# Moving the first output projection of an attention and feed-forward kernel into its last attention units

## The chip, the cores and the metric

The kernel runs on one core of a Trainium2 chip. The time is that of one execution on the device, in microseconds (us). Each core has a matrix engine (TensorE, PE in the profile, with its weight loads as PEld), a vector engine (VectorE, DVE), a scalar engine (ScalarE, ACT), a general engine (GpSimd, POOL) and SyncE (SP), which here issues nearly all DMA transfers. Each engine works through its own instructions in order and waits on semaphores for the others.

## What is computed

One cross-attention layer and one feed-forward layer with ternary weights, each added to its input. Cut to what matters:

```
x  = x + attn(layernorm(x), ctx)          # x 16x100x512, ctx 16x361x256
  q = rmsnorm(x Wq), k = rmsnorm(ctx Wk), v = ctx Wv     # 16 heads of 128
  o = softmax(q k' / sqrt(128)) v
  attn = o Wo                             # Wo 2048x512
x  = x + ffn(layernorm(x))
  bitlinear(a, w): a = fwht(a) (Hadamard), per row rounded to 8-bit integers by its
      absolute maximum; w rounded to -1, 0, 1 times its mean magnitude; a w'
  gate, up = bitlinear(h, w_gate), bitlinear(h, w_up)    # 512 to 2048
  ffn = bitlinear(silu(gate) * up, w_down)               # 2048 to 512
```

## The kernel before

Products that need more than one fp32r pass are made from split operands: a matrix a is written as hi (a rounded to fp32r) and lo (a - hi), and three products hi*hi, hi*lo, lo*hi are summed in PSUM. ACT makes the hi part, DVE the lo part.

**queries** makes q for all tokens, in four groups of 400 tokens. Per group the normed x is transposed into four PSUM banks (psX), split into xT_hi and xT_lo (one buffer each), and each of the 16 heads h is twelve products into psQ[h % 2]. ACT reads each head twice (q_out, squares). xT of the next group is split at head 15 (high_xT on ACT, low_xT on DVE). Wq arrives in four pieces of 1 MB through two staging slots, split where SPLIT_AT says. The middle groups are a loop.

**attention** works in 64 units (16 batches, 4 heads each); units 61 to 63 have no keys left to make, since keys run 12 heads ahead. In a unit TensorE does, for h = 0 to 3, the scores of a head (psS), and in between the transposes of two heads' probabilities pr (psP, line 778), the gather psZ of two units' contexts, and at h = 2 the values product of two units earlier (line 803). The softmax chain of a head is psS, DVE's scaling with maximum (line 1030) and nb (1037), ACT's exponential (875), DVE's inverse sum ri (1019), ACT's pr (882). The factors of the keys, rk, go by DMA to POOL and back, a unit or two ahead (spread_rk on SP, rms on POOL). Two units run on after the last (64 and 65) to finish gathers and values. The first half of Wo, 8 heads, is loaded in units 60 and 62 into four small slots and split by POOL in units 62 and 63 into wk_hi and wk_lo, whose keys are done (split_wo). o of the first 128 tokens is loaded into o_in at unit 60.

**feed_forward** works on 13 tiles of 128 tokens. Its steps are a pipeline: step(i) does gate and up of tile i + 1, the projection's end and the norm of tile i + 2, and down of tile i. Step -2 is the first. Per tile: out_proj (16 heads of three products, into psA), the residual sum, norm and first half of the Hadamard rotation on DVE (xn, xr), TensorE's transposes (norm_T), xT split, rotate_in, scales, rounding (mag, q), q1_T, gate_up, silu and product on ACT and DVE (stage), rotations, hidden_T, rotate_hidden, rounding, a DMA transpose, and down. Before the first step ACT and DVE split o of tile 0 and the second half of Wo (high_wo; L1527, L1550), and TensorE does out_proj(0), the last heads of it behind the v_w semaphore. busy(bank, n) issues n products whose results nobody uses. Heads 0 to AHEAD - 1 (6) of the projection of tile t + 1 are done ahead of gate_up of tile t. The feed-forward weights (wt, 3 MB, already ternary) are loaded by SP behind Wo's second half, x, had and o of tile 1. At the end, y is a scaling by ACT (scale_down) and an addition by POOL (result).

## Time and profile before

| | |
|---|---|
| median of three runs | 1473.45 us (1469.47 to 1475.27) |
| the profiled execution | 1468.72 us, span 1466.8 us |
| PE busy | 1427.9 us, 97% of the span |
| PEld busy | 1225.7 us, 84% |
| DVE busy | 954.2 us, 65% |
| ACT busy | 947.1 us, 65% |
| POOL busy | 524.0 us, 36% |
| queries, attention | about 0 to 188, 188 to 1048 us |
| feed-forward | about 1049 to 1467 us |

The profile is of one execution. Its timeline lists the instructions of an engine with start, length, and, where the engine stood idle before one, how long and what ended that. A matmul's length is modelled and overlaps the next, so the distance of two starts is what one costs in a row of many. A wait on several semaphores is put down to the one that came last.

### The profile page before, as it was taken

To read this page: it belongs to the slowest core of one execution; us is meant where nothing else is said; L and a number is where in the kernel's file an instruction comes from. 1 tells how busy PE (TensorE), PEld (TensorE's weight loads), DVE (VectorE), ACT (ScalarE), POOL (GpSimd) and SP (SyncE) were. 2 spreads that over 40 slices of the span, in tenths; PEclk is the share of its full clock that TensorE was granted. 3 is DMA by queue.
4 is the path that set the end of the run, shared out by engine and by line. 5 is a ranking of instruction groups with operands and counts; after the bars stand their busy time and mean duration, and the time that the engine had idled before them with its cause. 6 is when DMAs were issued, how large, how long until landed. Compare 5 with 4: busy or idle time off the path is not lost. (4 is left out here: it accounts for less than half of the span.)

```text
span 1466.8 us, 30515 instructions
## 1 busy us (share of the span) xinstructions
PE 1427.9 (97%) x8997; PEld 1225.7 (84%) x8997; DVE 954.2 (65%) x2464; ACT 947.1 (65%) x2069; POOL 524.0 (36%) x323
## 2 busy tenths in 40 slices
PE   8999989999999999999999999999899999999998
PEld 8888868999999989989999999998767677767765
DVE  5312056677777777777777777766467677767774
ACT  4556568878888878888788888887433334333432
POOL 0033324433322233323332333334244555555533
PEclk9999999999999999999999999999999999999999
DMA  7767723343444434343344434335533222322211
GB/s 238 215 180 195 206 78 85 103 110 106 116 125 117 120 105 116 112 130 110 106 122 124 115 110 115 105 83 140 158 118 88 71 57 64 95 69 57 64 32 40
DMA packets 187783, 165.07 MB, mean 113 GB/s; under 512 B 111040, under 2 KB 162256, under 8 KB 185872
## 3 DMA queue, kind: packets, MB, share of 16 engines
q1 hardware_dynamic: 180752, 151.21, 37.7%
q10 hardware_dynamic: 6912, 12.59, 2.7%
q8 instruction: 36, 0.59, 0.2%
q14 instruction: 83, 0.68, 0.2%
HBM read 123.44 MB, written 33.14 MB: 107 GB/s over the span
## 5 line engine op out<-in xcount | busy, mean ns | idle before, releaser
L707 POOL TENSOR_TENSOR rk_sp<-ms_sp,neg_half 76x10 f32<-76x10 f32 (+1 forms) x128 | 244.2, 1925 | 594.0 <-DMA ms_sp<-ms 594.0
L1030 DVE CUSTOM_DVE_ANT_0 sc<-psS,rk 100x361 f32<-100x361 f32 x256 | 136.3, 532 | 106.6 <-PE psS L765 82.9
L882 ACT ACTIVATE pr<-ex,ri 100x361 f32<-100x361 f32 x256 | 152.8, 597 | 81.5 <-DVE ri L1019 81.3
L875 ACT ACTIVATE ex<-sc,nb,rq 100x361 f32<-100x361 f32 x256 | 175.2, 684 | 8.5 <-DVE nb L1037 8.4
L741 PE MATMUL psK<-cT_hi,wk_hi 128*128 128x362 f32 x512 | 169.9, 332 | 1.7 <-DVE k_lo L1000 1.7
L863 ACT ACTIVATE k_hi<-psK 128x362 fp32r<-128x362 f32 x256 | 120.8, 472 | 76.1 <-PE psK L741 75.0
L741 PE MATMUL psK<-cT_lo,wk_hi 128*128 128x362 f32 x512 | 167.7, 328 | 0.0
L741 PE MATMUL psK<-cT_hi,wk_lo 128*128 128x362 f32 x512 | 167.7, 328 | 0.0
L1000 DVE TENSOR_TENSOR k_lo<-psK,k_hi 128x362 fp32r<-128x362 f32 x256 | 134.4, 525 | 6.7 <-ACT sq L869 5.4
L790 PE MATMUL psZ<-pT_hi,cK_hi 120*128 120x400 f32 (+1 forms) x384 | 132.8, 346 | 0.0
L790 PE MATMUL psZ<-pT_hi,cK_lo 120*128 120x400 f32 (+1 forms) x384 | 132.3, 344 | 0.0
L790 PE MATMUL psZ<-pT_lo,cK_hi 120*128 120x400 f32 (+1 forms) x384 | 132.3, 344 | 0.0
L803 PE MATMUL psNV<-z,wv_sb 128*128 128x100 f32 x1024 | 124.9, 275 | 1.4 <-issue 1.4
L803 PEld LDWEIGHTS psNV<-z,wv_sb 128*128 128x128 f32 x1024 | 119.4, 192 | 2.0 <-issue 2.0
L778 PEld LDWEIGHTS psP<-ident,pr 100*120 100x120 f32 (+1 forms) x768 | 79.7, 165 | 49.2 <-issue 27.7
L869 ACT ACTIVATE sq<-psK 128x362 f32<-128x362 f32 x256 | 118.7, 464 | 0.0
L778 PE MATMUL psP<-ident,pr 100*120 100x100 f32 (+1 forms) x768 | 96.9, 262 | 8.3 <-ACT pr L882 8.1
L1011 DVE TENSOR_TENSOR pT_lo<-psP,pT_hi 121x600 fp32r<-121x600 f32 x128 | 99.0, 774 | 4.2 <-ACT pT_hi L890 3.0
L741 PEld LDWEIGHTS psK<-cT_hi,wk_hi 128*128 128x128 f32 x512 | 96.5, 188 | 6.3 <-DVE k_lo L1000 5.1
L329 PE MATMUL psQ<-xT_hi,wq_hi 128*128 128x400 f32 x256 | 90.9, 355 | 7.0 <-ACT sq L406 5.9
L1019 DVE RECIPROCAL ri<-rs 100x1 f32<-100x1 f32 x256 | 41.3, 161 | 86.0 <-ACT ex L875 74.7
L1454 ACT ACTIVATE hT_hi<-psT 128x512 fp32r<-128x512 f32 x52 | 29.7, 596 | 104.4 <-PE psT L1364 104.4
(177 smaller groups left out, 3582.9 us busy)
## 6 DMA issues: line engine op xcount, KB each, us to landing
rk<-rk_dram SPq DMA_DIRECT2D x64, 564.1 KB
o_in<-o_dram SPq DMA_DIRECT2D x13, 1024.0 KB, 6.0
q_dram<-q_out SPq DMA_DIRECT2D x64, 200.0 KB, 4.4
q_in<-q_dram SPq DMA_DIRECT2D x64, 200.0 KB, 4.9
o_dram<-o SPq DMA_DIRECT2D x64, 200.0 KB, 5.3
stage<-in_w_ff SPq DMA_DIRECT2D x12, 1024.0 KB, 6.7
w_in<-in_w_ff ACTq DMA_DIRECT2D x48, 256.0 KB, 3.1
cT_in<-in_ctxT SPq DMA_DIRECT2D x16, 361.0 KB, 5.0
```

The lines of the kernel that those rows point to most:

```text
L707: nc.gpsimd.tensor_tensor(rk_sp[:, cols], ms_sp[:, cols], neg_half[0:HG * SKR, :].to_broadcast([HG * SKR, n]), op=ALU.pow).then_inc(g_rk, 1)
L741: last = nc.tensor.matmul(psK[h % 2][:, 0:SKP], w[:, c, col:col + D], x[:, slot, c, :], start=(n == 0), stop=(n == 3 * CC - 1))
L778: last = nc.tensor.transpose(psP[0:KW[i], k, i * SQ:(i + 1) * SQ], pr[:, 2 * half + k, KO[i]:KO[i] + KW[i]], ident[0:SQ, 0:SQ])
L790: last = nc.tensor.matmul(psZ[c][:, 0:UQ], w[0:KW[i], slot, i, c * P:(c + 1) * P], x[0:KW[i], j % 2, i, :], start=(n == 0), stop=(n == 8))
L803: last = nc.tensor.matmul(psNV[:, h * SQ:(h + 1) * SQ], wv_sb[:, c, col:col + D], z[:, j % 2, c, h * SQ:(h + 1) * SQ], start=(c == 0), sto ...
L863: nc.scalar.activation(k_hi[:, j, h, :], psK[h % 2][:, 0:SKP], ACT.Copy)
L869: nc.scalar.activation(sq[:, j % 2, h, :], psK[h % 2][:, 0:SKP], ACT.Square).then_inc(a_k, 1)
L875: nc.scalar.activation(ex[:, h % 2, :], sc[:, h % 2, :], ACT.Exp, bias=nb[:, h % 2:h % 2 + 1], scale=rq[:, j % 2, h:h + 1], accum_out=rs[: ...
L882: nc.scalar.activation(pr[:, h, :], ex[:, h % 2, :], ACT.Copy, scale=ri[:, h % 2:h % 2 + 1]).then_inc(a_pr, 1)
L1000: nc.vector.tensor_tensor(k_lo[:, j, h, :], psK[h % 2][:, 0:SKP], k_hi[:, j, h, :].bitcast(F32), ALU.subtract).then_inc(v_klo, 1)
L1011: nc.vector.tensor_tensor(two_heads(pT_lo, j, half), psP[0:KW[0], :, 0:3 * SQ].rearrange("p k (i q) -> p k i q", q=SQ), two_heads(pT_hi, j ...
L1030: nc.vector.tensor_tensor_reduce(out=sc[:, h % 2, :], in0=psS[0:SQ, 0:SK], in1=rk[:, j % 2, h, :], scale=1.0, scalar=-3.0e38, op0=ALU.mult ...
```

## The change

1. The projection of tile 0 moves out of the feed-forward stage into attention units 62 to 65, into psK's first bank, which becomes a bank that all stages share (bank0, psA afterwards). o of tile 0 is split there in four parts (high_o on ACT, low_o on DVE, unit 62) into the storage of cT and a new tile.
2. All of Wo is loaded and split in the attention stage. Heads 0 to 7 go to wk_hi and wk_lo, by POOL, from unit 61 on; heads 8 to 15 go to the keys' ring (ring_hi, ring_lo, whose storage is the keys' of attention and part of the queries' Wq and xT), hi by ACT in units 63 to 65, lo by POOL. There are nine slots, five of them in sq. On SP, o_in, x of tile 0 and the first four loads of Wo now stand ahead of unit 62's q and factors; five more stand between the two halves of unit 63's factors. o of tile 1 is loaded at unit 63.
3. The feed-forward stage starts with the residual of tile 0. Step -2 on TensorE interleaves heads 0 to 9 (FIRST) of tile 1's projection with tile 0's norm_T, rotate_in and q1_T; the 27 + 5 fillers there go. The weights' DMAs stand behind had and x of tile 1. Tile 0's transposes go to psT[0].
4. At the end, down of tile 11 moves ahead of the fillers, which are 13 for 27, and the last result is one DVE instruction, with no moving of residuals behind it.
5. In the queries, xT has two buffers and is split at heads 12 and 15; Wq's second piece is split at head 1 for head 0; the group loops are written out.

The diff, cut to its core:

```diff
-        SPLIT_AT = {0: 1, 2: 2, 4: 3, 8: 4, 10: 5}
+        SPLIT_AT = {1: 1, 2: 2, 4: 3, 8: 4, 10: 5}
+        XT_AT = {12: (0, 1), 15: (2, 3)}
...
-            with act.Fori(1, G - 1) as g:
+            for g in range(1, G - 1):
...
+        WO_HI_AT = {(UNITS - 3, 1): range(0, 4), **{(UNITS - 2, h): (4 + h,) for h in range(HG)}}
+        WO_LO_AT = {(UNITS - 1 + i // HG, i % HG): (8 + i,) for i in range(H // 2)}
+        WO_ACT_AT = {(UNITS - 1, 0): (8,), (UNITS - 1, 1): (9,), (UNITS - 1, 2): (10, 11), (UNITS - 1, 3): (12,),
+                     (UNITS, 0): (13,), (UNITS, 1): (14,), (UNITS, 2): (15,)}
+        OUT_AT = {(UNITS - 2, 0): (0,), (UNITS - 2, 2): (1, 2), (UNITS - 1, 0): (3,), (UNITS - 1, 1): (4, 5), (UNITS - 1, 2): (6, 7),
+                  (UNITS, 0): (8, 9), (UNITS, 1): (10,), (UNITS, 2): (11, 12), (UNITS + 1, 1): (13,), (UNITS + 1, 2): (14, 15)}
+        O_PARTS = [(0, 4), (4, 8), (8, 11), (11, H)]
...
+                if isinstance(u, int) and u == UNITS - 1:
+                    sp.wait_ge(p_ss, UNITS)
+                    for i in range(4, 9):
+                        load_wo(i)
                 sp.wait_ge(g_rk, powers)
...
+            def first_out(h):
+
+                if h == 0:
+                    pe.wait_ge(a_k, HEADS)
+                    pe.wait_ge(v_klo, HEADS)
+                part = [k for k, (lo, hi) in enumerate(O_PARTS) if lo <= h < hi][0]
+                pe.wait_ge(v_of, part + 1)
+                pe.wait_ge(g_wlo, h + 1)
+                o_hi, o_lo = (p[part][:, h - O_PARTS[part][0], :] for p in o_parts)
+                hi, lo = (w[h // 8][:, h % 8, :] for w in (wo_hi, wo_lo))
+                for i, (w, m) in enumerate(((o_hi, hi), (o_hi, lo), (o_lo, hi))):
+                    nc.tensor.matmul(psK[0][:], w, m, start=(h == 0 and i == 0), stop=(h == H - 1 and i == 2))
...
-            for i in range(PIECES):
-                sp.dma_start(slots[i].rearrange("p (h n) -> p h n", h=2), wo_v[PIECES + i]).then_inc(d_wo[i], 16)
-            sp.dma_start(x_in[:], x[0:TT, :]).then_inc(d_x, 16)
             sp.dma_start(stage[:, 1, 0:HC * HB].rearrange("p (c n) -> p c n", c=HC), had_in.rearrange("(c p) n -> p c n", p=P)
                          ).then_inc(d_had, 16)
-            for i in range(2):
-                sp.wait_ge(d_stored[i], 16 * B * NG // 2)
-            load_o(1, TT)
+            load_x(1, TT)
             for w in range(3):
                 sp.dma_start(wt[:, w, :, :].bitcast(BF16), wt_dram[w * WC:(w + 1) * WC].rearrange("c p n -> p c n")
                              ).then_inc(d_wt, 16)
...
             def step(i):
+                if isinstance(i, int) and i == -2:
+                    out_proj(1, range(0, 3))
+                    norm_T(0)
+                    out_proj(1, range(3, 5))
+                    rotate_in(0)
+                    out_proj(1, range(5, 9))
+                    q1_T(0)
+                    out_proj(1, range(9, FIRST))
+                    return
...
-                if isinstance(i, int) and i == TILES - 2:
-                    busy(psA, 27)
+                late = isinstance(i, int) and i == TILES - 2
+                if late:
+                    down(i, 0, front)
+                    down(i, 1, front)
+                    busy(psA, 13)
...
-            busy(psT[0], 6)
+            busy(psT[1], 8)
             pe.wait_ge(v_ident, 1)
-            out_proj(0, range(0, AHEAD))
...
+            def last_result(t):
+
+                dve.wait_ge(p_down, t + 1)
+                dve.wait_ge(d_out, t * 16)
+                dve.wait_ge(g_old, (t + 2) * 2)
+                dve.wait_ge(v_scale[1], 5 * t + 5)
+                nc.vector.scalar_tensor_tensor(y[:], psF[:], ald[:], x1[:, 0, :], ALU.mult, ALU.add).then_inc(v_y, 1)
```

TensorE in unit 62, from a head's scores (psS2) to the next head's, before:

```order
L765 MATMUL psS2<-k_hi,q_hi 100x362
L765 MATMUL psS2<-k_lo,q_hi 100x362
L765 MATMUL psS2<-k_hi,q_lo 100x362
L778 MATMUL psP<-ident,pr 121x100
L778 MATMUL psP<-ident,pr 120x100 x2
```

and after; the new rows' names are those of the storage, wk for Wo and cT for o:

```order
L814 MATMUL psS2<-ring_lo,q_hi 100x362
L814 MATMUL psS2<-ring_hi,q_lo 100x362
L867 MATMUL bank0<-wk_hi,cT_hi 128x512
L867 MATMUL bank0<-wk_lo,cT_hi 128x512
L867 MATMUL bank0<-wk_hi,cT_lo 128x512
L827 MATMUL psP<-ident,pr 121x100
L827 MATMUL psP<-ident,pr 120x100 x2
```

One head of the projection stands between the scores and the transposes of pr.

DVE from the start of the feed-forward stage to the rotated norm of tile 0, before:

```order
L1541 CAST ident_b<-ident 128x128
L1545 TENSOR_TENSOR o_lo<-o_in,o_hi 128x512 x4
L1550 TENSOR_TENSOR wo_lo<-stage,wo_hi 128x1024 x2
L1550 TENSOR_TENSOR wo_lo<-mag,wo_hi 128x1024 x2
L1555 CAST had<-stage 128x512
L1571 TENSOR_TENSOR x<-psA,x_in 128x512
L1573 BN_STATS st<-x 128x6
L1576 BN_AGGR mv<-st 128x2
L1578 TENSOR_SCALAR ve<-mv 128x1
L1695 TENSOR_TENSOR o_lo<-o_in,o_hi 128x2048
L1584 TENSOR_SCALAR xn<-x,mv,rstd 128x512
L1592 TENSOR_TENSOR xr<-xn 128x256 x2
```

and after:

```order
L1631 CAST ident_b<-ident 128x128
L1658 TENSOR_TENSOR x<-bank,x_in 128x512
L1660 BN_STATS st<-x 128x6
L1663 BN_AGGR mv<-st 128x2
L1665 TENSOR_SCALAR ve<-mv 128x1
L1635 TENSOR_TENSOR o_lo<-o_in,o_hi 128x512 x2
L1671 TENSOR_SCALAR xn<-x,mv,rstd 128x512
L1679 TENSOR_TENSOR xr<-xn 128x256 x2
L1640 CAST had<-stage 128x512
L1635 TENSOR_TENSOR o_lo<-o_in,o_hi 128x512 x2
L1683 TENSOR_TENSOR xT_lo<-psT,xT_hi 128x512
```

Nine instructions stood ahead of the statistics' end, five do now; two of tile 1's four o_lo pieces stand between the statistics and the norm, two and had's rounding behind it.

TensorE behind the last tile's projection, from gate_up (psB<-wt) on, before:

```order
L1352 MATMUL psB<-wt,q1T 128x512 x32
L1392 MATMUL psA<-wk_hi 128x512 x27
L1364 MATMUL psT0<-ident,stage3 128x128 x4
L1364 MATMUL psT1<-ident,stage3 128x128 x4
L1384 MATMUL psF<-wt,q2T 128x512 x16
```

and after:

```order
L1445 MATMUL psB<-wt,q1T 128x512 x32
L1477 MATMUL psF<-wt,q2T 128x512 x16
L1485 MATMUL bank0<-wk_hi 128x512 x13
L1457 MATMUL psT0<-ident,stage3 128x128 x4
L1457 MATMUL psT1<-ident,stage3 128x128 x4
```

Down (psF) of tile 11 went from behind the transposes of the hidden tile to ahead of the fillers.

## Rows read from the trace of the kernel before

**Rows 1.** Windows: us, busy time (instructions) of PE, PEld, DVE, ACT, POOL, clock, DMA:

```profile
1077.90:1434.90 357.00, 352.27 (x1931) 247.74 (x1930) 257.78 (x483) 135.63 (x181) 190.83 (x120) 1.00 0.26 63
```

**Rows 2.** Timeline, queries: start, length, engine, line, operation, [idle before, what ended it]:

```profile
26.24 1.92 ACT L363 ACTIVATE wq_hi<-stage 128x2048 fp32r<-128x2048 f32 x1 [1.05 <-DMA stage<-in_wq]
...
100.13 0.42 PE L329 MATMUL psQ<-xT_hi,wq_hi 128*128 128x400 f32 x1 [0.57 <-DVE xT_lo L469]
...
142.07 0.42 PE L329 MATMUL psQ<-xT_hi,wq_hi 128*128 128x400 f32 x1 [0.52 <-issue]
```

**Rows 3.** Timeline of PE, units 62 to 65: transposes of pr, last values product:

```profile
1016.34 0.80 PE L778 MATMUL psP<-ident,pr 100*121 100x100 f32 x6 [0.52 <-ACT pr L882]
...
1020.71 0.80 PE L778 MATMUL psP<-ident,pr 100*121 100x100 f32 x6 [0.96 <-ACT pr L882]
...
1036.55 0.80 PE L778 MATMUL psP<-ident,pr 100*121 100x100 f32 x6 [1.04 <-ACT pr L882]
...
1045.78 2.00 PE L803 MATMUL psNV<-z,wv_sb 128*128 128x100 f32 x16 [0.71 <-issue]
```

**Rows 4.** Timeline of PE, first and 24th product of the projection of tile 0:

```profile
1050.93 0.47 PE L1305 MATMUL psA<-wk_hi,o_hi 128*128 128x512 f32 x1
...
1056.23 0.39 PE L1305 MATMUL psA<-wk_hi,o_lo 128*128 128x512 f32 x1
```

**Rows 5.** Timeline, DVE in unit 62; ACT and DVE splitting o later:

```profile
1016.72 0.21 DVE L1037 TENSOR_SCALAR nb<-mx,rq 100x1 f32<-100x1 f32 x1
...
1049.31 2.20 ACT L1533 ACTIVATE o_hi<-o_in 128x512 fp32r<-128x512 f32 x4 [1.00 <-PEq L527]
...
1049.98 2.50 DVE L1545 TENSOR_TENSOR o_lo<-o_in,o_hi 128x512 fp32r<-128x512 f32 x4
```

**Rows 6.** Timeline, POOL at unit 63's factors; DVE and ACT beside POOL's split:

```profile
1015.47 3.70 POOL L707 TENSOR_TENSOR rk_sp<-ms_sp,neg_half 76x10 f32<-76x10 f32 x2 [11.38 <-DMA ms_sp<-ms]
...
1021.11 0.96 DVE L993 TENSOR_TENSOR q_lo<-q_in,q_hi 128x400 fp32r<-128x400 f32 x1
1022.00 1.23 DVE L995 COPY rq<-rq_all 100x4 f32<-100x4 f32 x1
...
1023.32 0.60 ACT L882 ACTIVATE pr<-ex,ri 100x361 f32<-100x361 f32 x1 [1.31 <-DVE ri L1019]
```

**Rows 7.** Timeline, first feed-forward step, chain from the residual to gate_up:

```profile
1063.38 0.69 DVE L1571 TENSOR_TENSOR x<-psA,x_in 128x512 f32<-128x512 f32 x1 [1.35 <-PE psA L1305]
...
1065.48 0.55 POOL L1233 TENSOR_TENSOR rstd<-ve,neg_half 128x1 f32<-128x1 f32 x1 [14.80 <-DVE ve L1578]
...
1066.23 2.51 DVE L1695 TENSOR_TENSOR o_lo<-o_in,o_hi 128x2048 fp32r<-128x2048 f32 x1 [0.90 <-ACT o_hi L1447]
...
1070.35 0.66 PE L1313 MATMUL psA<-ident,xr 128*128 128x128 f32 x4 [0.88 <-DVE xr L1592]
...
1071.67 0.69 DVE L1596 TENSOR_TENSOR xT_lo<-psA,xT_hi 128x512 fp32r<-128x512 f32 x1 [1.38 <-ACT xT_hi L1461]
...
1077.91 7.23 PE L1352 MATMUL psB<-wt,q1T 128*128 128x512 fp8e4 x32
```

**Rows 8.** Windows, as rows 1, while the feed-forward weights were loading:

```profile
1060.00:1065.00 5.00, 5.00 (x23) 3.79 (x22) 3.29 (x6) 2.52 (x4) 0.00 (x0) 1.00 1.12 336
```

**Rows 9.** Timeline, second step: DVE's sum across halves, PE's hidden transposes:

```profile
1090.54 1.22 DVE L1680 TENSOR_TENSOR stage<-stage 128x1024 f32<-128x1024 f32 x1
...
1091.82 1.09 PE L1364 MATMUL psT<-ident,stage 128*128 128x128 f32 x8
```

**Rows 10.** Timeline of the end: down, rotation, first hT_lo pair, last addition:

```profile
1442.84 3.62 PE L1384 MATMUL psF<-wt,q2T 128*128 128x512 fp8e4 x16
...
1446.11 0.47 PE L1374 MATMUL psB<-had,hT_hi 128*128 128x256 f32 x1
...
1443.24 1.29 DVE L1559 TENSOR_TENSOR hT_lo<-psT,hT_hi 128x512 fp32r<-128x512 f32 x2 [1.38 <-ACT hT_hi L1454]
...
1463.08 1.26 POOL L1272 TENSOR_TENSOR y<-y,x 128x512 f32<-128x512 f32 x1 [12.94 <-ACT y L1487]
```

More of the change, by code:

```diff
@@ L268, in _ @@
             group(0, True, False)
-            with pool.Fori(1, G - 1) as g:
+            for g in range(1, G - 1):
                 group(g, False, False)
@@ L346, in _ @@
             group(0, True, False)
-            with pe.Fori(1, G - 1) as g:
+            for g in range(1, G - 1):
                 group(g, False, False)
             group(G - 1, False, True)
-            busy(psX[0], wq_hi[:, 0, 0:P], xT_hi[:, 0, :], 4)
+            busy(psX[0], wq_hi[1][:, 0, 0:P], xT_hi[0][:, 0, :], 4)
             squares(G - 1, NG - 1)
-            busy(psX[0], wq_hi[:, 0, 0:P], xT_hi[:, 0, :], 6)
+            busy(psX[0], wq_hi[1][:, 0, 0:P], xT_hi[0][:, 0, :], 6)
             factors(G - 1)
@@ L496, in _ @@
             split_first(0)
-            low_xT(0)
+            for c in range(DC):
+                low_xT(0, c)
             split_first(1)
             group(0, True, False)
-            with dve.Fori(1, G - 1) as g:
+            for g in range(1, G - 1):
                 group(g, False, False)
@@ L1205, in _ @@
                              ).then_inc(d_wt, 16)
-            load_x(1, TT)
+            for i in range(2):
+                sp.wait_ge(d_stored[i], 16 * B * NG // 2)
             load_o(2, 2 * TT)
@@ L1407, in step @@
                     busy(psA, 27)
-                if real(i):
+                if real(i) and not late:
                     down(i, 0, front)
@@ L1508, in step @@
                     high_o(i + 3)
[L1509 removed]
+                if real(i) and not last_tile(i):
                     scale_down(i)
@@ L1541, in _, with low_o @@
             nc.vector.tensor_copy(ident_b[:], ident[:]).then_inc(v_ident, 1)
-            for k in range(NO):
+            def low_o(k):
                 heads = slice(k * OH, (k + 1) * OH)
@@ L1692, in step @@
                     residual(i + 2)
-                if isinstance(i, int) and i == -2:
-                    dve.wait_ge(a_o, NO + 1)
-                    nc.vector.tensor_tensor(o_lo[:], o_in[:], o_hi[:].bitcast(F32), ALU.subtract).then_inc(v_o, 1)
+                first = isinstance(i, int) and i == -2
+                if first:
+                    low_o(0)
+                    low_o(1)
                 if real(i + 1):
```

282 lines of the change are left out of this document (162 added, 120 removed).

## Prediction

> **What bounds the kernel now.** I read the stretches first. In the feed-forward stage TensorE is busy 352.27 of 357.00 us at full clock [rows 1], and the stages before it look alike, so TensorE's own order of work sets the time nearly everywhere. A gain can only come from places where TensorE waits, or does work that counts for nothing. The timeline of TensorE shows three such places. In the queries a few short waits remain [rows 2]. In the last attention units the keys are finished, and TensorE waits for the softmax chain before each turn of the probabilities and before each values product [rows 3]. The largest is the seam between attention and feed-forward: the last values product starts at 1045.78 and runs 2.00 us, the first useful product of the next stage starts at 1050.93 [rows 3, 4], and the first gate and up product at 1077.91 [rows 7]. The 27 us between these two are the projection of tile 0 followed by a chain of small steps with only fillers beside it. At the end of the kernel 27 fillers stand ahead of the last but one down (the order in the part on the change), which the chain then passes [rows 10].
>
> **Queries.** Splitting xT in two places with two buffers removes the wait for DVE xT_lo, 0.57 us, and written-out loops remove the one that nothing in the profile explains, 0.52 us [rows 2]. A loss is possible: the split of Wq's second piece moves behind the first head's two reads on ACT, about 1 us, so the DMA of the fourth piece goes out later; before, ACT got it at 26.24 after a wait for that DMA [rows 2]. The loss is nothing if the queue stays full and at most the moved split's own stretch, 2 to 3 us, if it passes through whole. The timeline lists no wait of TensorE right behind the 26.24 split, so I take 0.4: **-0.7**, bounds -1.5 and +1.5.
>
> **Last attention units.** The projection of tile 0, 16 heads of three products, is now done here. From 1050.93 to 1056.23 there are 23 starts, 0.23 us each [rows 4], so a head costs 0.69 us and all 16 cost 11.0. The heads stand ahead of five probability turns and two values products. The waits there are 0.52 (twice, the other 0.55), 0.96 (twice, the other 0.93), 1.04 and 0.71 (twice) [rows 3]. A product's modelled length overlaps the next by about 0.17, so the seven waits can hold 5.4 + 1.2 = 6.6 us. Filling without any loss costs 11.0 - 6.6 = 4.4 us.
>
> It isn't perfect. The first head in unit 62 needs the first four heads of o split. ACT can start that when the probabilities are done that let the turn begin at 1016.34 [rows 3], and takes a quarter of 2.20; DVE gets to it after its factor at 1016.72 + 0.21 = 1016.9 and takes a quarter of 2.50 [rows 5]. So the head starts near 1017.6, and the turn begins near 1018.25, 1.9 us late. Walking the other slots (0.3, 0.0, 1.4, 0.3, 0.2, 0.7, 0.5, 0.7 and 0.5 us: heads less the wait that they fill; two slots stand at no wait) adds 4.6: +6.5. ACT's five later splits and POOL's 24 Wo operations have the time of two units more than before and stay beside this.
>
> There is a price for the parts of o and Wo that run together. In unit 62, DVE's q_lo took 0.96 and the copy of rq, four elements, 1.23 us beside POOL's split, and ACT then waited 1.31 us for the inverse sum [rows 6]. Three of the four new o_lo pieces fall in the same company. An o_lo piece of 0.62 hides under the exponential; stretched by as much as that wait it doesn't. The bounds are nothing (before, that wait moved no turn: from 1016.34 to 1036.55 two units took 10.1 us each [rows 3]) and 3 x 1.3 = 3.9. I take 0.5, nearer to the case in which the wait was absorbed. **Attention +7.0**, bounds +4.4 and +10.4.
>
> The Trainium skill, SBUF — State Buffer, section "Who interferes with whom", says that a VectorE instruction with two SBUF inputs and a GpSimd one that reads SBUF exclude each other, and the later one waits for the whole of the other. By it each o_lo piece could meet a Wo split and lose the whole of that, and the term would be the upper bound above; by the row it is the 0.5. The stretched q_lo agrees with the rule.
>
> **Start of the feed-forward.** Let t be its first instant (1049.3 before, 1.5 us after the last values product ends). DVE is free about 0.7 later and adds x at once, since the projection is in the bank. From that add to POOL's power took 1065.48 - 1063.38 = 2.1, the power 0.55 [rows 7]: t + 3.4. Two o_lo pieces (1.25) end at t + 4.0 and cover most of the power. Norm and half rotation took 1.6 (o_lo's end, 1066.23 + 2.51, to TensorE's turn at 1070.35) [rows 7]: t + 5.6. TensorE's three heads of tile 1 start when the first o_lo piece is there and end at t + 5.4, just in time. xT_lo followed the turn by 1.32 [rows 7], t + 6.9, but now stands behind the rounding of had and two more pieces (1.7), t + 7.3. From xT_lo to gate_up took 6.24, of which 0.6 was TensorE still at heads of tile 1 [rows 7]. So gate_up is ready near t + 13.0 where it was t + 28.6: **-15.6**.
>
> Gate_up also needs all three of the ff weights' DMAs. They go out after the load of x for tile 1, which waits for the add: t + 1.4 and later. Had, x and the weights are 3.6 MB; at the 336 GB/s of the stretch in which they ran before [rows 8] that is 10.7 us, and with about 1.5 us to start t + 13.5. **+0.5**, bounds 0 (the chain is later anyway) and, at a rate a third lower, +5.
>
> Four heads more of tile 1 (2.8 us) are done before gate_up than before. I count nothing for them: in the next step TensorE's turn of the hidden tile, at 1091.82, starts as DVE's sum across halves ends, 1090.54 + 1.22 [rows 9]. TensorE will be early there and wait. From there on the tiles run as before.
>
> **End.** Down for tile 11 moves before 13 fillers in place of after 27. It takes 3.3 (1442.84 to 1446.11 [rows 10]) and 13 fillers 3.0, so TensorE, done with the last gate_up at the end of the stretch of [rows 1], 1434.9, is through at 1441.2, and the hidden turn before 1442.84 stays where DVE's sum puts it. The rotation at 1446.11 then waits only for the first hT_lo, 1443.24 + 0.65 = 1443.9 [rows 10]: -2.2. The last result is one DVE pass in place of an ACT pass and POOL's add of 1.26 [rows 10]: -1.2. The last stretch is all one chain, so both count: **-3.4**, bounds -2.2 and -3.6.
>
> **Sum.** -0.7 + 7.0 - 15.6 + 0.5 - 3.4 = **-12.2 us**. The profiled execution took 1468.7, its span 1466.8; the sum makes it 1456.5. The median of the three runs is 1473.45, 4.7 above that execution, and I take the difference as it stands: **1461.2 us**. The best ends together give -18, the worst -1; added as independent errors they leave about -17 to -6.
>
> **Rivals.**
> First, the seam moves rather than closes (chance 0.17): the heads in the units fill nothing, since ACT, with some 5 us more in units 62 and 63, is late at each turn by what TensorE was late before, and the weights' DMAs land late. Then attention costs its 10.4 and the weights 3 more than I took: -6.2, 1467.3. For it speaks that ACT waits under 1.4 us at a time in these units [rows 6]; against it that TensorE is pushed back by 7 us, and ACT with it.
> Second, exclusion on the last units (0.04), which would make the kernel **slower**. POOL's 24 operations on Wo now lie in units 61 to 64, beside four o_lo pieces, and the probabilities' chain passes DVE at every head. Each meeting that lands on the chain costs what the inverse sum lost, about 1.1 us [rows 6]. If all 24 did, it would be +26 us and the time near 1487; it decides from the twelfth meeting on. Before, 16 operations ran there and one was seen to cost this, and it was absorbed.
> Third, the first projection waits for its Wo (0.04): 24 operations, four of them ahead of the keys' factors for unit 63, push those factors late by about their length, 7.7 us. The loss would be some 5 us, 1466. Against it: before, POOL began the same factors at 1015.47, after 11.38 us of waiting for their DMA [rows 6], and the four pieces end at about that instant.
> Fourth, the edits gain more than I say (0.10): no loss in the queries, waits filled whole and the weights early: -17, 1456.
>
> **How the numbers follow.** The forecast itself has 0.65. Its own range is 1456 to 1466; with the spread of the medians (the three runs lie 6 us apart) and the first and fourth rivals, 1453.5 to 1468.5 leaves out two in ten. A measurement of this kernel tells about 0.5%, 7.4 us, from no change, so faster begins below 1466.1. The forecast and the fourth rival lie there but for their upper edge, the first and third lie half on either side or beyond: faster 0.79, same 0.16, slower 0.05.
>
> **What would show it.** Right: the last values product starts some 7 us later than 1045.78 (less the queries' gain), and the waits of [rows 3] are gone but one before the first head in unit 62; gate_up of tile 0 stands about 13 us behind the stage's start, with no long wait for a DMA before it; in the next step TensorE waits 2 to 3 us more for DVE before the hidden turn; from the first gate_up to the end of the last it is 357 us as before [rows 1]; from the last gate_up to the end it is 3.4 us shorter. Wrong: a first head near 1020 or later; gate_up waiting for the weights by several us; tiles that take longer; new waits for the keys' factors at units 62 or 63; or a loss in the first group of queries above 1.5 us.

## The result and the profile after

| | before | after |
|---|---|---|
| median | 1473.2 us (6 runs, 1469.47 to 1475.27) | 1464.6 us (6 runs, 1461.03 to 1465.72) |
| ratio, with 95% interval | | 0.9942 (0.9926 to 0.9959) |
| the profiled execution, its span | 1468.72, 1466.8 us | 1464.46, 1462.7 us |
| PE busy | 1427.9 us | 1422.4 us |

The change makes the kernel 8.6 us faster, 0.58% (by the interval 0.4 to 0.7%). The two profiled executions lie only 4.3 us apart, because that of before lies below all six timed ones and that of after at the median.

The timeline of after, TensorE: the first head of the projection in unit 62, a turn in unit 63, the last values product, the first product of tile 1's projection, the normed tile's turn and the first gate and up product. They answer to [rows 3], [rows 4] and [rows 7].

```profile
1019.31 0.47 PE L867 MATMUL bank<-wk_hi,cT_hi 128*128 128x512 f32 x1 [1.97 <-DVE cT_lo L1095]
...
1031.69 0.80 PE L827 MATMUL psP<-ident,pr 100*121 100x100 f32 x6 [1.21 <-ACT pr L946]
...
1055.12 1.92 PE L852 MATMUL psNV<-z,wv_sb 128*128 128x100 f32 x16
...
1061.63 0.47 PE L1398 MATMUL bank<-wk_hi,o_hi 128*128 128x512 f32 x1 [0.92 <-DVE o_lo L1635]
...
1064.10 0.66 PE L1406 MATMUL psT<-ident,xr 128*128 128x128 f32 x4
...
1073.46 4.87 PE L1445 MATMUL psB<-wt,q1T 128*128 128x512 fp8e4 x14 [2.27 <-DMA wt<-wt_dram]
```

The last values product starts 9.3 us later than in [rows 3] and gate_up 4.5 us earlier than in [rows 7]. The feed-forward stage begins at t = 1058.60; gate_up stands at t + 14.9 where it stood at t + 28.6. Ahead of gate_up TensorE waits 2.27 us for the weights.

The second step, which answers to [rows 9]: TensorE's hidden turn and the first rotated product.

```profile
1089.04 1.09 PE L1457 MATMUL psT<-ident,stage 128*128 128x128 f32 x8 [2.49 <-DVE stage L1767]
...
1091.48 0.58 PE L1467 MATMUL psB<-had,hT_hi 128*128 128x256 f32 x1 [1.35 <-DVE hT_lo L1644]
```

What the prediction didn't have is in the granted clock. Windows of after: us, busy time (instructions) of PE, PEld, DVE, ACT, POOL, clock, DMA. The first answers to [rows 1]; the next show both first feed-forward steps, the last two the start of the queries.

```profile
1073.40:1434.40 361.00, 354.50 (x1917) 249.06 (x1918) 258.44 (x483) 135.32 (x181) 190.72 (x120) 0.99 0.26 64
1072.00:1074.00 2.00, 0.54 (x2) 0.28 (x3) 0.00 (x0) 0.00 (x0) 0.00 (x0) 0.92 1.20 300
1074.00:1076.00 2.00, 2.00 (x6) 0.75 (x5) 0.00 (x0) 0.00 (x0) 0.00 (x0) 0.50 0.60 142
...
1092.00:1094.00 2.00, 2.00 (x12) 2.00 (x11) 1.97 (x5) 0.62 (x1) 0.75 (x1) 0.50 0.00 0
1094.00:1096.00 2.00, 2.00 (x11) 2.00 (x11) 0.99 (x2) 0.60 (x1) 2.00 (x1) 0.50 0.00 0
...
12.00:14.00 2.00, 2.00 (x13) 2.00 (x12) 1.82 (x3) 2.00 (x6) 0.00 (x0) 0.53 0.44 162
14.00:16.00 2.00, 2.00 (x14) 2.00 (x13) 2.00 (x4) 0.77 (x1) 0.00 (x0) 0.62 0.00 0
```

Three times the clock falls from its upper level (1.00, 2.4 GHz) to the lower (0.50, 1.2 GHz), each time right behind idle time of TensorE: 2.27 us at 1071 to 1073, then 2.49 and 1.35 us around the hidden turn (the transposes of the hidden tile), and 1.91 us at 8.4 to 10.3 ahead of the first transposes of x. Gate_up of tile 0 takes 8.55 us (1073.46 to 1082.01) where before took 6.88 (1077.91 to 1084.79); from the hidden turn to the next gate_up it is 15.84 us for 14.34. From the first gate_up to the end of the last it is 361 us, not 357.

The end, from the chain that ended last (start, length, what; the x27 are fillers, L1477 is down, L1775 the new last result), with the span's end at 1462.7:

```profile
1449.06 6.17 PE bank L1485 x27
1455.22 0.60 issue
1455.82 3.63 PE psF L1477 x16
1459.45 0.02 issue
1459.47 0.75 DVE y L1775
```

From the last gate_up, 1427.48, to the end it is 35.2 us; before, from 1428.04 to 1466.8, it was 38.8.

### The profile page after: what moved, and what is told of

Same layout as the page of the kernel before. It is cut to its first block and busy times, and to the rows that moved or that the text cites. A ratio compares the mean times of both kernels' runs of the same rounds, so it can differ in the third digit from the quotient of the medians.

```text
span 1462.7 us, 30158 instructions
## 1 busy us (share of the span) xinstructions
PE 1422.4 (97%) x8953; PEld 1223.1 (84%) x8953; DVE 951.7 (65%) x2464; ACT 947.3 (65%) x2075; POOL 528.6 (36%) x328
## 5 line engine op out<-in xcount | busy, mean ns | idle before, releaser
L1445 PE MATMUL psB<-wt,q1T 128*128 128x512 fp8e4 x416 | 95.7, 384 | 3.2 <-DMA wt<-wt_dram 2.3
L814 PE MATMUL psS<-ring_hi,q_hi 128*100 128x362 f32 x256 | 92.0, 359 | 4.6 <-DVE mx L1119 4.6
L927 ACT ACTIVATE ring_hi<-bank 128x362 fp32r<-128x362 f32 x128 | 60.2, 470 | 50.2 <-PE bank L790 50.2
L1445 PEld LDWEIGHTS psB<-wt,q1T 128*128 128x128 bf16 x416 | 38.9, 98 | 57.2 <-issue 18.1
L790 PE MATMUL bank<-cT_hi,wk_hi 128*128 128x362 f32 x256 | 85.3, 333 | 1.0 <-DVE ring_lo L1082 1.0
L790 PE MATMUL psK<-cT_hi,wk_hi 128*128 128x362 f32 x256 | 85.0, 332 | 0.6 <-DVE ring_lo L1082 0.6
L968 ACT ACTIVATE pT_hi<-psP 121x600 fp32r<-121x600 f32 x128 | 83.9, 655 | 0.7 <-PE psP L827 0.6
L814 PE MATMUL psS<-ring_lo,q_hi 128*100 128x362 f32 x256 | 84.1, 329 | 0.0
```

Of the source, the lines that this page charges most:

```text
L790: last = nc.tensor.matmul(psK[h % 2][:, 0:SKP], w[:, c, col:col + D], x[:, slot, c, :], start=(n == 0), stop=(n == 3 * CC - 1))
L814: last = nc.tensor.matmul(psS[0:SQ, 0:SKP], w[:, j % 2, cols], x[:, j, h, :], start=(i == 0), stop=(i == 2))
L968: nc.scalar.activation(two_heads(pT_hi, j, half), psP[0:KW[0], :, 0:3 * SQ].rearrange("p k (i q) -> p k i q", q=SQ), ACT.Copy).then_inc(a_ ...
L1445: last = nc.tensor.matmul(psB[:, 2 * (j % 2) + k, :], q1T[:, c, :], wt[:, k, c, j * DIM:(j + 1) * DIM], start=(c == 0), stop=(c == DC - 1))
```

## The experiments

All traces in one table, each number a difference of two starts in one trace's timeline. "Head 0" is the start of the first q_out in the queries; "0 to 6" the distance of the seventh's to it; "61 to 62" and "61 to 65" the distances between the values products in those units (V61 is the one in unit 61, V62 the next, and so on); "V to G" from the last of these (V65) to the first gate_up (G0); "G0 to G1" and "G1 to G12" between the gate_ups of tiles 0, 1 and 12; "end" from that of tile 12 to the end of the span. Times are us; "clock" is the mean granted clock of the traced execution. Each ratio below is to the kernel before, executed beside it (medians 1469.51, 1471.32 and 1470.09 us). E4_no_heads and e9_gates were executed once and have none.

| kernel | head 0 | 0 to 6 | 61 to 62 | 61 to 65 | V to G | G0 to G1 | G1 to G12 | end | clock |
|---|---|---|---|---|---|---|---|---|---|
| before | 16.36 | 18.28 | 10.13 | 34.57 | 32.13 | 28.25 | 321.88 | 38.8 | 0.999 |
| b1_before | 16.71 | 17.87 | 10.12 | 34.60 | 31.96 | 28.24 | 321.86 | 38.7 | 0.999 |
| after | 18.45 | 20.59 | 12.43 | 42.37 | 18.34 | 31.42 | 322.60 | 35.2 | 0.995 |
| a2_after | 17.64 | 20.14 | 13.97 | 43.93 | 18.42 | 31.26 | 323.26 | 35.2 | 0.993 |
| e1_fillers | 17.83 | 20.23 | 12.50 | 42.53 | 18.92 | 28.14 | 322.84 | 35.2 | 0.998 |
| e2_tail_undone | 16.74 | 20.33 | 12.45 | 42.44 | 19.24 | 29.70 | 322.59 | 37.5 | 0.996 |
| e3_split_at_0 | 16.40 | 17.70 | 13.99 | 42.98 | 17.02 | 28.71 | 322.75 | 35.2 | 0.998 |
| e4_no_heads | 21.05 | 20.34 | 13.54 | 40.66 | 18.06 | 28.77 | 322.89 | 35.2 | 0.993 |
| e5_weights_first | 16.42 | 20.30 | 13.34 | 43.52 | 16.29 | 29.16 | 322.76 | 35.2 | 0.998 |
| e6_pool_gate | 17.00 | 20.43 | 12.44 | 42.17 | 17.92 | 30.18 | 322.63 | 35.1 | 0.998 |
| e7_head_moved | 16.72 | 20.08 | 11.84 | 41.98 | 18.03 | 28.81 | 323.27 | 35.2 | 0.996 |
| e9_gates | 16.26 | 20.10 | 14.49 | 43.50 | 19.12 | 31.01 | 322.68 | 35.2 | 0.994 |
| c1_all | 16.16 | 17.92 | 14.01 | 43.69 | 16.04 | 28.19 | 322.86 | 35.2 | 0.999 |
| c2_all | 17.69 | 17.96 | 10.99 | 41.02 | 16.55 | 28.10 | 322.25 | 35.1 | 1.000 |

**The kernel before once more** (no edit).

> The kernel before, unchanged, profiled again. The one profiled execution of before lies 4.7 us below the median of its three runs, and its granted clock was 0.999 where all six runs of the changed kernel show 0.994 to 0.996. In the changed kernel's trace the opening fillers of TensorE end at 8.35, it idles 1.91 us and the clock is 0.50 from about 12 to 15.5; in before's trace they end at 9.31, it idles 0.51 and the clock stays at 1.00. Theory: which of the two happens at the start changes from run to run in either kernel and is worth 2 us (first head's q_out at 16.36 or near 18.4); then most of these executions have a clock below 0.999 and are 2 us or more above 1468.7. Rival: the start is the changed kernel's own doing; then every execution of before shows 0.999 and the first head at 16.4.

Its ten runs have a median of 1468.77 us, ratio 0.9997 (0.9987 to 1.0006), clocks of 0.998 to 1.000; the thirteen of before beside them have 0.997 to 1.000. The new trace shows 1.72 us of idle time ahead of the first transposes and still a clock of 1.00 with head 0 at 16.71. So neither theory holds as it stands: the fall at the start stands in neither trace of before, but it isn't the changed kernel's own doing either, since in six of the eight variants below that leave the start as it is head 0 stands between 16.26 and 17.00. The mean granted clock of all executions tells the two apart: 0.9955 over the six of a2_after, 0.9990 over the eleven of before beside it. By estimate that is 0.0035 of 1461 us, 5.1 us of TensorE's work lost, some of it under waits.

**Fillers in the first two steps.** The first line stands at the end of step -2, ahead of the first gate_up, the others around the hidden turn.

```diff
+                    busy(psF, 10)
...
+                if isinstance(i, int) and i == -1:
+                    busy(psF, 13)
                 if real(i + 1):
                     hidden_T(i + 1, 0)
                     hidden_T(i + 1, 1)
+                if isinstance(i, int) and i == -1:
+                    busy(psF, 6)
```

> The changed kernel with products whose results nobody uses in the places where TensorE stood idle in the first two feed-forward steps: 10 ahead of the first gate_up, 13 ahead of the hidden turn and 6 behind it in the second step. Theory: the idle stretches made the granted clock fall to 0.50 from 1073.9 to 1076.5 and from 1091 to 1097, which cost gate_up 8.55 in place of 6.88 us (1.7) and the rotations 15.84 in place of 14.34 us (1.5); with fillers both are back and the kernel is 3.2 us faster. Rival: the chains on DVE set these stretches and the clock only fills their waits: no change. Second rival: the fillers end later than the data and cost up to 1 us.

Windows of e1_fillers, with the columns of those above, over gate_up and over the second step:

```profile
1071.00:1079.00 8.00, 7.44 (x35) 3.37 (x35) 2.52 (x4) 2.12 (x4) 2.09 (x2) 1.00 0.25 60
1083.00:1099.00 16.00, 15.32 (x99) 13.20 (x98) 13.57 (x31) 6.65 (x9) 9.70 (x5) 1.00 0.27 73
```

The clock stays at 1.00 and G0 to G1 is 28.14 us, as before the change, for 31.42: the theory holds in the trace, to the 3.3 us. The ratio, 0.9945 (0.9928 to 0.9961), shows nothing of it: the medians don't bear the gain out. The weights landed late in this trace (15.4 us behind the stage's start, V to G 18.92), and the spread of the other stretches is as large as the gain. The second rival has a small part: the 13 fillers reach past the end of DVE's sum at 1085.50, and the hidden turn starts at 1085.82, 0.3 behind it. The stretch is as short in c1_all and c2_all (28.19 and 28.10), the kernels in which the same fillers stand around the hidden turn.

**The end undone.**

```diff
                 if late:
-                    down(i, 0, front)
-                    down(i, 1, front)
-                    busy(psA, 13)
+                    busy(psA, 27)
```

> The changed kernel with down of tile 11 again behind the turn of the hidden tile and 27 fillers ahead, as in before; the single-pass last result stays. By the prediction this gives back 2.2 us of the 3.4 at the end. Rival: the order is hidden behind the chain on DVE and only the single pass counted; then the end is as long as before this edit and the time is the same.

The end is 37.5 us, 2.3 more than with the edit (35.2) and 1.3 less than before (38.8). That is the prediction's 2.2 and 1.2. The ratio, 0.9946 (0.9930 to 0.9963), is too coarse for it.

**Wq's second piece split ahead of the first head.**

```diff
-        SPLIT_AT = {1: 1, 2: 2, 4: 3, 8: 4, 10: 5}
+        SPLIT_AT = {0: 1, 2: 2, 4: 3, 8: 4, 10: 5}
```

> The changed kernel with the second piece of Wq split ahead of the first head again, as in before. By the prediction the later split costs 0.4 us (bounds 0 and 2 to 3). By the traces the first group lost another 2.0 us between its second and its seventh head (q_out of head 6 at 39.04, 4.4 later than before, of which 2.1 are the clock at the start): if the later split is the cause, this kernel's head 6 stands 2.3 us or less behind before's and the kernel gains up to 2 us. Rival: the loss is in the stores of q that share the queue with the loads, and the place of the split is worth under 0.5.

ACT in the first group, timeline of after and then of e3_split_at_0: the split of Wq's fourth piece and the q_out of head 6.

```profile
29.02 1.91 ACT L369 ACTIVATE wq_hi<-stage 128x2048 fp32r<-128x2048 f32 x1 [3.00 <-DMA stage<-in_wq]
...
39.04 0.59 ACT L405 ACTIVATE q_out<-bank,gprod 128x400 f32<-128x400 f32 x1 [2.80 <-DMA q_dram<-q_out]
```

```profile
25.23 1.92 ACT L369 ACTIVATE wq_hi<-stage 128x2048 fp32r<-128x2048 f32 x1 [0.49 <-DMA stage<-in_wq]
...
34.10 0.60 ACT L405 ACTIVATE q_out<-bank,gprod 128x400 f32<-128x400 f32 x1 [3.06 <-PE psQ L337]
```

From head 0 to head 6 it is 17.70 us, and 17.9 in the other two kernels with this line, for 20.1 to 20.6 in the nine with the later split: 2.4 us. The ratio is 0.9923 (0.9906 to 0.9940), with that of e5_weights_first the lowest of the single edits, though its interval overlaps that of after. The later split frees the staging slot later, the fourth piece lands later, and its split stands ahead of q_out on ACT. Measured from head 0, the second piece's split ends 3.0 us later in after than in e3_split_at_0, and 2.4 of these come through to head 6.

**The projection's products left out.** Only the last head's first product stays; the waits for o and Wo stay too.

```diff
-                for i, (w, m) in enumerate(((o_hi, hi), (o_hi, lo), (o_lo, hi))):
-                    nc.tensor.matmul(psK[0][:], w, m, start=(h == 0 and i == 0), stop=(h == H - 1 and i == 2))
+                if h == H - 1:
+                    nc.tensor.matmul(psK[0][:], o_hi, hi, start=True, stop=True)
```

> The changed kernel without the products of the first output projection in attention units 62 to 65 but for one, so the first tile's result is wrong. All splits of o and Wo stay. Theory: TensorE's own extra work is what the last values product is late by (it starts 60.4 us after the one of unit 57 at 994.7 in the changed kernel, 7.8 us more than before); then the last units are as short as before within 0.5 us. Rival: the splits on ACT, DVE and POOL hold up the chain of the probabilities; then 1 us or more of the 7.8 stays without the products.

TensorE's timeline in units 62 and 63:

```profile
1021.98 1.36 PE L827 MATMUL psP<-ident,pr 100*121 100x100 f32 x6 [2.42 <-DVE cT_lo L1095]
...
1027.88 0.77 PE L827 MATMUL psP<-ident,pr 100*121 100x100 f32 x6 [1.06 <-ACT pr L946]
...
1035.29 1.28 PE L827 MATMUL psP<-ident,pr 100*121 100x100 f32 x6 [2.18 <-ACT pr L946]
```

Without 47 of the 48 products units 61 to 65 still take 40.66 us, 6.1 more than before. The rival wins in the first two units: from V61 to V63 it is 25.99 us, 20.22 before and 25.53 in after, so there the arrival of o_lo and of the probabilities holds TensorE up and the products only fill that time. From V63 to V65 the theory holds: 14.67 us, 14.35 before and 16.84 in after, so there the products cost 2.2 of the 2.5 us. Part of the 6.1 is the clock: the two turns of 1.36 and 1.28 us took 0.80 in [rows 3], behind 2.42 and 2.18 us of idle time. At the 1.5 us that such a fall costs in c1_all below, the two are at most 3 us of it (an estimate). So this run overstates what the splits alone cost, and the share of each stays open.

**The weights ahead of x.**

```diff
-            load_x(1, TT)
             for w in range(3):
                 sp.dma_start(wt[:, w, :, :].bitcast(BF16), wt_dram[w * WC:(w + 1) * WC].rearrange("c p n -> p c n")
                              ).then_inc(d_wt, 16)
+            load_x(1, TT)
```

> The changed kernel with the DMAs of the feed-forward weights ahead of the load of x for tile 1, which waits for the residual. Theory: the weights land 1.4 us earlier and more, since x no longer stands ahead; gate_up of tile 0, 14.9 to 15.8 us behind the stage's start in three traces, starts at 12.6 to 13.0, where the chain is ready; without the idle stretch the clock stays at 1.00 there: 2 to 4 us faster. Rival: the transfer rate sets it and the other loads of the start (o of tiles 2 and 3) share it: no change.

The first gate_up of this kernel:

```profile
1069.97 0.81 PE L1445 MATMUL psB<-wt,q1T 128*128 128x512 fp8e4 x3 [0.23 <-DMA wt<-wt_dram]
```

The first gate_up in TensorE's timeline stands 12.8 us behind the stage's start (1057.17) and waits 0.23 us; in the nine changed kernels with the old order it is 13.5 to 15.8 us. The clock is 1.00 throughout gate_up. The theory holds for this stretch. The ratio, 0.9924 (0.9907 to 0.9942), is some 2 to 2.5 us below those of after and a2_after, inside the theory's 2 to 4, but the intervals overlap.

**POOL held back once.**

```diff
+                if i == 6:
+                    pool.wait_ge(v_rq, UNITS)
```

> The changed kernel with POOL waiting, before its seventh piece of Wo, until DVE has q_lo and the copy of rq for the last unit. Theory: DVE's q_lo (0.98 us) and copy of four elements (1.25 us) in unit 62 are stretched by POOL's splits beside them, ACT's pr then waits 2.23 us for the inverse sum and TensorE's turn at 1031.69 waits 1.21 us; apart, they take 0.56 and 0.16, that turn comes about 1 us earlier, and the kernel is about 1 us faster. Rival: TensorE waits elsewhere instead, for Wo's seventh head that is split later: no change or up to 1 us slower.

In after, POOL's split, DVE's two instructions and ACT's pr in unit 62; they answer to [rows 6].

```profile
1026.35 1.50 POOL L762 TENSOR_TENSOR wk_lo<-sq,wk_hi 128x512 fp32r<-128x512 f32 x1
...
1025.72 0.98 DVE L1075 TENSOR_TENSOR q_lo<-q_in,q_hi 128x400 fp32r<-128x400 f32 x1
1026.62 1.25 DVE L1077 COPY rq<-rq_all 100x4 f32<-100x4 f32 x1
...
1027.98 0.60 ACT L946 ACTIVATE pr<-ex,ri 100x361 f32<-100x361 f32 x1 [2.23 <-DVE ri L1108]
```

In e6_pool_gate the same two of DVE, and the later piece of o_lo with POOL's split beside it:

```profile
1024.07 0.57 DVE L1077 TENSOR_TENSOR q_lo<-q_in,q_hi 128x400 fp32r<-128x400 f32 x1
1024.55 0.16 DVE L1079 COPY rq<-rq_all 100x4 f32<-100x4 f32 x1
...
1027.88 1.52 DVE L1097 TENSOR_TENSOR o_rest_lo<-o_in,o_rest_hi 128x640 fp32r<-128x640 f32 x1
...
1027.41 1.31 POOL L764 TENSOR_TENSOR wk_lo<-sq,wk_hi 128x512 fp32r<-128x512 f32 x1
```

The copy of four elements ends at 1027.87 where POOL's split ends at 1027.85, and takes 0.16 without it. The piece of o_lo ends at 1029.40, 0.68 behind POOL's 1028.72. So the stretch is one waiting for the other's end. The Trainium skill, SBUF — State Buffer, section "Who interferes with whom", says that a DVE instruction with two SBUF inputs contends with one of POOL that reads SBUF, and that a DVE copy does so in its two-port modes. The trace agrees for o_lo; which mode the copy of rq ran in it doesn't show. The stretch moved but wasn't removed: TensorE's wait in unit 63 went from 1.21 to 0.99 us, the ratio is 0.9944 (0.9927 to 0.9960). What holds that turn now is the same meeting one instruction later: the inverse sum stands behind the stretched o_lo on DVE, and ACT's pr waits 1.42 us for it.

```profile
1029.51 0.60 ACT L948 ACTIVATE pr<-ex,ri 100x361 f32<-100x361 f32 x1 [1.42 <-DVE ri L1110]
```

The rival is right for the time but not for its reason: no wait of TensorE for POOL's Wo stands in this timeline.

**All five together.** The three edits above, the fillers of the second step, and at the very start 29 fillers for 22 and 9 for 11.

```diff
-            busy(psQ[0], weights["ones"][:], weights["ones"][:], 22)
+            busy(psQ[0], weights["ones"][:], weights["ones"][:], 29)
```

> The changed kernel with five edits together: Wq's second piece split ahead of the first head, seven more fillers at the very start and two fewer behind the transposes, the feed-forward weights ahead of x, POOL's wait as in the run before, and fillers in the second feed-forward step around the hidden turn. If each does what its theory says: 3.0 for the split, up to 2 for the start (only in executions in which the clock fell there), 3 for the weights, 1 for POOL, 1.5 for the fillers, about 9 us below the changed kernel, ratio to before near 0.988. Rival: the gains overlap in the same waits, and it is not better than the changed kernel with the split alone, 0.9923.

Ratio 0.9899 (0.9883 to 0.9914), 1455.81 us beside 1471.32: 6 us better than after by the ratios, for the 9 hoped for. The trace shows one reason, TensorE's first head in unit 62 and the six transposes behind it:

```profile
1014.22 0.47 PE L869 MATMUL bank<-wk_hi,cT_hi 128*128 128x512 f32 x1 [1.96 <-DVE cT_lo L1097]
...
1014.99 1.10 PE L829 MATMUL psP<-ident,pr 100*121 100x100 f32 x6
```

The six took 0.80 us in [rows 3]. Behind 1.96 us of idle time the clock falls here too; its mean from 1010 to 1018 is 0.82, and units 61 to 62 take 14.01 us. The same wait in after (1.97) had no fall behind it and 12.43 us; in a2_after, the same kernel, it had one and 13.97 us. So one fall costs 1.5 us here, and whether it comes changes from execution to execution: of the ten traces with this wait five have it (a2_after, e3, e4, e9, c1_all) and five don't.

**The first head moved**, and **POOL held back three times**.

```diff
-        OUT_AT = {(UNITS - 2, 0): (0,), (UNITS - 2, 2): (1, 2),
+        OUT_AT = {(UNITS - 2, 2): (0, 1, 2),
```

> The changed kernel with the first head of the projection moved from unit 62's first place to its third (heads 0, 1 and 2 stand there together). In the changed kernel TensorE waits 1.97 us for DVE's cT_lo ahead of that head and does the turn behind it late; in two variants the clock also fell to 0.50 behind this wait (units 61 to 62 between values products: 14.0 in place of 12.4 us, before 10.1). Theory: without the wait the turn comes 2.2 us earlier, the third place costs 0.8 more, and the distance of the two values products is 11.0 to 11.3 with no fall of the clock: 1.2 us faster than without the fall, 2.8 than with it. Rival: the chain of the probabilities (ACT and DVE also split o there) is late by as much; then the distance stays at 12 or more.

```profile
1014.61 0.80 PE L827 MATMUL psP<-ident,pr 100*121 100x100 f32 x6 [0.51 <-ACT pr L946]
...
1020.71 0.80 PE L827 MATMUL psP<-ident,pr 100*121 100x100 f32 x6 [0.56 <-ACT pr L946]
```

The 1.97 us are gone, the turn waits 0.51 for pr, and units 61 to 62 take 11.84 us for 12.4 or 14.0. It is 0.5 to 0.8 more than the theory said, and those 0.56 us are a new wait for pr behind three heads: a part of cT_lo took 1.70 us in this trace. Ratio 0.9935 (0.9913 to 0.9957), not to be told from after's 0.9942.

```diff
+                if i in (5, 7):
+                    pool.wait_ge(v_of, {5: 2, 7: 4}[i])
+                if i == 6:
+                    pool.wait_ge(v_rq, UNITS)
```

> The changed kernel with three waits on POOL, so that each of its splits of Wo in unit 62 starts behind one of DVE's: the sixth piece behind the second part of o_lo, the seventh behind the copy of rq, the eighth behind the fourth part of o_lo. With the seventh alone held back, rq took 0.16 us and q_lo 0.57, but a part of cT_lo took 1.66 and o_rest_lo 1.49 beside other splits. Theory: it is the meeting of two instructions that stretches, wherever it falls; apart, all of these take 0.54 to 0.85, ACT's waits for the inverse sum of 1.4 to 2.2 us go, and units 61 to 63 (values product to values product, 12.4 + 13.1) shrink by 1 to 2 us. Rival: POOL, later by 2 to 3 us, makes the heads of the projection wait for Wo: they stay as long.

This one is inconclusive. Rq and q_lo took 0.15 and 0.56, but two parts of cT_lo still 1.13 and 1.32, and the first head waited 2.45 us with a fall of the clock behind it. ACT's longest wait for the inverse sum in unit 62 was 0.93 us for 2.23, and TensorE's wait in unit 63 was 0.29 us for 1.21, but it is 0.29 in e3_split_at_0 too, where the copy of rq took 1.25. Units 61 to 62 took 14.49, 62 to 63 12.19; the sum, 26.7 with one fall of the clock in it, is no better than after's 25.5 without one and near a2_after's 27.1 with one.

**The changed kernel again, and all edits.**

> The changed kernel, unchanged, on the same chip as the next run, for comparison: ratio to before 0.994.

> All edits of the combined kernel, with the three waits on POOL in place of one and with the first head moved to its third place. If both theories hold: 2.8 us for the head (in the combined kernel the clock fell behind that wait) and 1 to 2 for the waits, so some 4 us below the combined kernel, ratio to before 0.987, 10 us or more below the changed kernel. Rival: one stretch of the chain takes the place of the other, ratio 0.990 as before.

A2_after: 1461.81 us, ratio 0.9938 (0.9923 to 0.9953), clocks 0.993 to 0.998. C2_all: 1450.73 us beside 1470.09 for before on the same chip, **ratio 0.9870 (0.9853 to 0.9886)**, 19.4 us faster than before and 11.1 faster than the changed kernel. Windows of c2_all over the start, unit 62 and the first two feed-forward steps:

```profile
8.00:20.00 12.00, 10.12 (x76) 9.77 (x75) 9.74 (x19) 6.57 (x10) 1.03 (x1) 1.00 0.53 187
1010.00:1018.00 8.00, 7.49 (x47) 7.00 (x46) 5.43 (x17) 6.85 (x15) 7.62 (x8) 1.00 0.79 258
1066.00:1098.00 32.00, 30.98 (x167) 21.71 (x167) 21.91 (x41) 11.31 (x15) 14.98 (x9) 1.00 0.37 75
```

The clock never falls there, though TensorE waits 1.88 us ahead of the first transposes of x, and the four executions have 0.999 to 1.000. Units 61 to 62 take 10.99 us, 0.9 more than before with three heads in them. The three waits on POOL did not do their part: rq took 1.26 us again and ACT waited 2.23 us for the inverse sum, since POOL's sixth piece came just then. Its gate, the second part of o_lo, had been open since 1018.19, so it followed the fifth piece at 1019.98 with no wait; the gate held nothing back here. Of the 4.3 us over c1_all by the ratios, 2.7 stand in units 61 to 65, where the head was moved and the fall of the clock is gone.

## Why the prediction was right or wrong

The sign, the range and the place were right; the time was 1464.6 for 1461.2, a gain of 8.6 for 12.2. The mechanism was right too: the seam closes by more than the attention units grow. Two of the terms were too favourable, attention and tiles. The terms, by the means of all traces that leave a stretch as the change made it against the two of before:

| step | predicted | measured | how |
|---|---|---|---|
| Queries | -0.7 | -0.4 | head 0 +0.9, heads 0 to 6 +2.2, head 6 to the last q_out -3.5 |
| Attention | +7.0 | +9.1 | last q_out to V61 +0.7, V61 to V65 +8.4 (42.96 for 34.58) |
| Start, with the weights | -15.1 | -13.8 | V to G, 18.27 for 32.04 |
| Tiles | 0 | +2.6 | G0 to G1 +1.65, G1 to G12 +0.91 |
| End | -3.4 | -3.6 | 35.18 for 38.74 |
| Sum | -12.2 | -6.1 | the medians say -8.6 and -8.3 |

The traced executions of before lie 4.5 and 1.8 us below the medians of their runs. Those of the changed kernel and its variants lie on both sides: after's at the median, a2_after's the slowest of six, e1's and e3's the fastest of four. So the traces understate the gain by about 2 us. The terms are to be read with that.

Some figures of the prediction's working don't add up, though the forecast itself does. The best ends together give -16.3 and not -18, the first rival's terms -5.8 and not -6.2, and -17 to -6 from 1473.45 is 1456 to 1467 and not 1466. No run shows the 1.5 us that the weights' DMAs were given to start; what was measured is under Start.

**Queries.** The sum was near by luck, since two errors cancel. The moved split was put at 0.4 since no wait of TensorE stood right behind the 26.24 split; it costs 2.4, within the 2 to 3 us that the text gave as its whole length. The wait shows at head 4, as ACT's 3.00 us for the fourth piece, and at head 5, as its 3.36 us for stores of q. From head 6 to the last q_out it is 145.4 us for 148.9, 3.5 less where 1.09 was forecast. TensorE's idle time in that stretch went from 5.3 us in before to 2.0 in after, of which the prediction counted two waits. Of the edits the two buffers and the written-out loops act there; which of them brings it wasn't tried. No run ties head 0's +0.9 to an edit: it changes with how long TensorE waits for the first normed x (up to 3.63 us, in e4_no_heads) and with the fall of the clock there, and it is +0.5 without e4_no_heads.

**Attention.** The step that rested on o_lo was near: the turn behind the first head stands 2.2 us later behind V61 than in before (7.33 for 5.13) where 1.9 was said. The walk over the slots failed at unit 63, where a wait of 1.21 us for pr stayed at 1031.69. The meeting of DVE and POOL, priced at 0.5, stands ahead of it: ACT's pr of 1027.98 is 2.23 us late, and ACT then works with a pause of 0.23 us up to the pr that the turn needs. Moving that meeting (e6_pool_gate) shortened the wait by only 0.2, but it put another in its place, so no run shows these units with no meeting and no fall of the clock, and the price stays open. That TensorE's products set these units is right for V63 to V65 and wrong for V61 to V63 (e4_no_heads). Of the miss, a fall of the clock is worth 1.5 us in half of the traces, and 0.7 us lie ahead of V61 (827.6 us from the last q_out for 826.9), where the prediction had no term; what costs them stays open.

**Start.** The chain is ready at t + 12.5 (q1T on ACT from 1070.48, 0.60 long) for the forecast's 13.0. The weights landed at t + 14.9 for 13.5. The rate was right or better (357 to 382 GB/s from 1066 to 1072, for 336), the time to reach it wasn't: from 1060 to 1064 the DMA ran at 241 and then 220 GB/s. The wait for x counted as well, since with the weights ahead of it gate_up came at t + 12.8. The forecast's order of the two ends, weights last by 0.5, was right and the 0.5 was 1.9. It also missed what a wait at this place does to the clock.

**Tiles.** "From there on the tiles run as before" is the step that failed most. It saw that TensorE would idle 2 to 3 us before the hidden turn (2.49) and gave that no price. Each of the idle stretches made the clock fall: 1.7 us in gate_up of tile 0 and 1.5 in the rotations in the profiled execution. E1_fillers shows that the 3.3 us are the clock's, since fillers alone bring them back in its trace. In before, ten heads of tile 1 stood between gate_up and the hidden turn; the change left six, and the prediction counted the four that moved ahead as nothing. The other 0.9 us, 0.08 for each of eleven tiles, are in all twelve traces of the changed kernel and its variants (322.25 to 323.27 for 321.9); their cause stays open.

**End.** Both parts as forecast.

**Rivals.** None took place as it was written. The attention term came near the first one's 10.4 in some traces (a2_after 9.3), in part through the clock and not through a late ACT alone. DVE and POOL met, as the second said, but at a few places, not twelve. The third didn't come: in after POOL starts unit 63's factors at 1017.31, having waited 0.45 us for their DMA, and no wait of TensorE for Wo shows in units 62 to 65. Of the signs of being wrong two came, a loss in the first group above 1.5 us (3.1 at head 6 in the mean) and longer tiles, and gate_up waited 2.27 us for the weights. All three are in the table above.

## What to carry to other kernels

Before removing fillers or filling a hole elsewhere, list the idle stretches that the change leaves on the matrix engine and put a price on each: here about 1.5 us if the clock falls behind it. The wait can be removed (the weights first, the head later) or filled; fillers bring the clock back but not the wait, and those that reach past the data cost the rest (0.3 us in e1_fillers). A split that frees a staging slot belongs ahead of work that can wait, because most of the next DMA's delay passes through (here 2.4 of 3.0 us).

## What the runs showed of the hardware

The granted clock fell to 0.50 behind idle stretches of TensorE of 1.55, 1.91, 1.96, 2.27, 2.45, 2.49 and 3.63 us, and didn't fall behind others of 1.31, 1.59, 1.72, 1.97, 2.36 and 3.17 us. Ahead of gate_up it fell behind 1.94 us in e6_pool_gate and 3.15 in e9_gates, and not behind 1.97 in e7_head_moved and 3.17 in e2_tail_undone. The same kernel at the same place did both: 1.97 us in unit 62 in after without a fall, and in a2_after with one. At the hidden turn, where 2.47 to 2.53 us of idle time and then, in eight of them, another 1.35 stand, it fell in all nine traces of the changed kernel and its variants without fillers there. So the length of a single stretch doesn't decide it. Two executions of one kernel can differ by several us, and the clock goes along with that: a2_after's six have clocks of 0.993 to 0.998, the slowest (1464.72 us) the lowest.

DVE's copy of four elements in units 61 and 62 took 1.23 to 1.27 us at least once in thirteen of the fourteen traces, always beside POOL's subtraction for a lo part and ending 0.02 to 0.04 behind it. Beside POOL's rounding for a hi part it took 0.57 or 0.58 in six traces, and 0.15 or 0.16 where none ran.
